# Gate softmax: eight of 32 row tiles of one half of the columns summed with the columns on partitions

## The reference

```
layer 0: x += codebook[argmin distance(gn(x), 1024 codes)]
layer 1: f, g, h = gn(x) @ Wf, Wg, Wh;  x += sigmoid(f g^T per image row) h
layer 2: x0, x1, x2 = gn(x) @ w1, w2, w3                     # one number per pixel each
         sim[n, m] = x0[n] * x1[m];  sm = softmax over n
         feats[m] = sum over n of x2[n] * sm[n, m]
         x += sigmoid(feats) * gn(x)
layer 3: q, k, v = gn(x) @ Wqkv; q softmax over 32, k softmax over 4096 pixels
         out = (k^T v) applied to q, @ w_out + b_out, layer norm;  x += out
```

## Time and profile before

| what | us |
|---|---|
| median of three runs | 5602.64 |
| span of the profiled execution | 5601.4 |
| TensorE busy | 5252.2 |
| VectorE busy | 4106.3 |
| ScalarE busy | 3978.2 |
| GpSimd busy | 1936.0 |

### The profile page before, as it was taken

The page is one execution under the profiler, slowest core; times in us unless marked ns, Lnnn a source line. Parts: engine busy times, 40 slices in busy tenths (PEclk is TensorE's granted clock), DMA queues, the critical chain, the costliest instruction groups (busy, mean ns, idle before and its releaser), DMA issues.

```text
span 5601.4 us, 113931 instructions
## 1 busy us (share of the span) xinstructions
PE 5252.2 (94%) x44520; PEld 2737.7 (49%) x44520; DVE 4106.3 (73%) x8674; ACT 3978.2 (71%) x6023; POOL 1936.0 (35%) x1594
## 2 busy tenths in 40 slices
PE   7799999999999999999999999999999999999996
PEld 3436445363553645446364453645436454463624
DVE  8467777776777777677777777777677777777726
ACT  1467867677785877868677675877858678686795
POOL 3225243342423424233352423424234242433403
PEclk9799999999999999999999999999999999999997
DMA  2010201102011020201102011020110102011000
GB/s 86 9 37 11 68 25 52 37 6 72 20 61 31 13 67 15 64 28 35 48 11 70 23 57 33 15 64 17 61 31 20 61 13 67 26 47 40 7 31 31
DMA packets 163253, 211.22 MB, mean 38 GB/s; under 512 B 13217, under 2 KB 146081, under 8 KB 162721
## 3 DMA queue, kind: packets, MB, share of 16 engines
q1 hardware_dynamic: 138144, 136.79, 7.6%
q0 software_dynamic: 24576, 67.14, 4.1%
HBM read 136.78 MB, written 67.11 MB: 36 GB/s over the span
## 4 chain that ended last, share of the span: by engine, by line
PE 66%; ACT 13%; DVE 11%; issue 6%; POOL 2%; DMA 1%; ACTq 0%; DVEq 0%; SPq 0%; POOLq 0%
PE PS L1195 33%; PE PS L1372 15%; PE PS L1363 6%; ACT n_x L529 3%; DVE stats L849 2%; PE PS L1471 2%; PE PS L1229 2%; PE PS L1253 2%; PE PS L1306 2%; ACT big L601 2%; ACT xin L529 2%; DMA quant_H<-emb_t,idx 1%; ACT work L568 1%; ACT attn L578 1%; ACT soft L601 1%
## 5 line engine op out<-in xcount | busy, mean ns | idle before, releaser
L601 ACT ACTIVATE big<-PS 128x1024 f32<-128x1024 f32 x1376 | 1365.8, 1024 | 460.3 <-PE PS L1363 398.9
L601 ACT ACTIVATE soft<-PS 128x1024 f32<-128x1024 f32 x672 | 676.2, 1024 | 353.9 <-PE PS L1363 346.3
L416 POOL DMA_INDIRECT quant_H<-emb_t,idx x512 | 487.4, 952 | 976.2 <-DVE idx L873 781.2
L1195 PE MATMUL PS<-e_hi,n_hi 128*128 128x512 f16 x2048 | 780.2, 381 | 17.3 <-DVE m L867 9.5
L1195 PE MATMUL PS<-e_hi,n_lo 128*128 128x512 f16 x2048 | 776.7, 379 | 0.0
L1195 PE MATMUL PS<-e_lo,n_hi 128*128 128x512 f16 x2048 | 776.7, 379 | 0.0
L1372 PE MATMUL PS<-big,w 128*4 128x512 f32 x5504 | 756.5, 638 | 0.0
L849 DVE BATCH_NORM_STATS2 stats<-XT 128x6 f32<-128x512 f32 x1024 | 651.7, 683 | 14.5 <-POOL XT L432 4.6
L873 DVE FIND_INDEX8 idx<-m,work 128x8 uint32<-128x1024 f32 x512 | 622.1, 1219 | 0.0
L1363 PE MATMUL PS<-rhs,lhs 12*128 12x512 bf16 x4096 | 557.6, 395 | 61.7 <-ACT big L601 38.8
L867 DVE CUSTOM_DVE_ANT_0 work<-PS,e_bias,m 128x512 f32<-128x512 f32 x512 | 384.0, 750 | 213.2 <-PE PS L1195 189.5
(11 more groups left out here) (208 smaller groups left out, 10799.7 us busy)
## 6 DMA issues: line engine op xcount, KB each, us to landing
xin<-x SPq DMA_DIRECT2D x128, 512.0 KB, 3.9
out<-yout SPq DMA_DIRECT2D x128, 512.0 KB, 2.9
quant_H<-emb_t,idx POOLq DMA_INDIRECT x512
XT<-emb SPq DMA_DIRECT2D x1, 1024.0 KB, 6.2
XT<-wh SPq DMA_DIRECT2D x1, 256.0 KB, 5.8
XT<-wqv SPq DMA_DIRECT2D x1, 256.0 KB, 5.8
XT<-wk SPq DMA_DIRECT2D x1, 128.0 KB, 5.8
w_sb<-w SPq DMA_DIRECT2D x1, 128.0 KB, 5.3
```

The lines of the kernel that those rows point to most:

```text
L416: nc.gpsimd.indirect_dma_start(quant[:, g % 2, u, :], None, emb_t, bass.IndirectOffsetOnAxis(ap=idx[:, t % (2 * GT), 0:1], axis=0),).then_ ...
L601: nc.scalar.activation(E[h % 3][:, z * 1024:(z + 1) * 1024], bank(2 * z, 2), ACT.Exp).then_inc(exped.sem, 1)
L1195: ins = mm(dst, a, b, start=first and j == 0, stop=last and j == 2)
```

## The change

For row tiles 24 to 31 and the second half of the columns (16 column tiles of 128), the products are computed the other way round. The columns m lie on the partitions and 1024 rows n along the free dimension.

- `HALVES` is 56 instead of 64: halves 56 to 63 (two fills, two exponentials, one group of sums each) fall away.
- `rows_out` (SyncE) writes the x0 and x2 values of the last 1024 rows from `rows3` to a DRAM buffer, in two DMAs. `rows_back` reads each back as a row spread over 128 partitions, into `x0_row` and `x2_row` (512 KB each).
- `bexp(im, i)`, 16 per image, on ScalarE: the exponential of `x0_row` with the column's x1 as scale and the negative maximum as bias, both pointers, into `EB`; the denominator comes from the accumulator.
- `bsum(im, i)`, 16 per image, on VectorE: `EB * x2_row`, and its sum is the numerator. All share the one buffer `EB`.
- `extremes` makes `negm`; `gate_chain` adds the 16 sums to those of the matmuls.
- `EB` is `o_x0` and the rows lie over `o_hi` and `o_lo`, the buffers of layer 3; the squares go to a small bf16 buffer; `pk` and `r3` lie over `yout`. `gated(0)` waits for the last `bsum`. `final_z` waits for `l3_qlo` of its own group in the last two groups.
- The lists of the loop on all engines are laid out anew. In the loop six `bexp` stand ahead of the next image's first `l0_norm` and ten behind it; ten `bsum` stand after the first `best`. In the search VectorE takes the next tile's first maximum ahead of the index of the tile before, and `stat1` of groups 5 and 6 and `add0(13)` come after the last index. In the last image `gated(0)` moves behind `gate_chain(0)`.

The diff, without most of the lists:

```diff
-HALVES = 2 * NT
+ROWS = 8
+SIDE = NT // 2
+HALVES = 2 * NT - ROWS
...
+    rows_d = nc.dram_tensor("rows_d", (B, 2, ROWS * P), F32)
...
-        o_hi = sb("o_hi", [P, 2, KC, GW], F16)
-        o_lo = sb("o_lo", [P, 2, KC, GW], F16)
+        o_both = sb("o_both", [P, 2 * GW * KC])
+        o_hi, o_lo = (o_both[:, i * KC * GW:(i + 1) * KC * GW].bitcast(F16).rearrange("p (s k n) -> p s k n", s=2, k=KC)
+                      for i in range(2))
+        x0_row, x2_row = o_both[:, 0:ROWS * P], o_both[:, ROWS * P:2 * ROWS * P]
+        EB = o_x0[:, :, :].rearrange("p k n -> p (k n)")
+        negm = sb("negm", [P, NT])
+        bden = sb("bden", [P, SIDE])
+        bnum = sb("bnum", [P, SIDE])
...
+            def rows_out(im):
+                sp.wait_ge(*rows_kept.after(im, 1))
+                for i in range(2):
+                    sp.dma_start(rows_d[im, i, :].rearrange("(q n) -> q n", q=2),
+                                 rows3[2 * i + 64:P:32, 1, :]).then_inc(rows_sent, 16)
+
+            def rows_back(im):
+                sp.wait_ge(rows_sent, 32 * (im + 1))
+                if im > 0:
+                    sp.wait_ge(*l3_qved.after(im - 1, NG - 1))
+                    sp.wait_ge(*l3_ked.after(im - 1, NG - 1))
+                for i, row in enumerate((x0_row, x2_row)):
+                    sp.dma_start(row, rows_d[im, i, :].partition_broadcast(P)).then_inc(rows_in, 16)
...
+            def bexp(im, i):
+                t = SIDE + i
+                if i == 0:
+                    act.wait_ge(rows_in, 32 * (im + 1))
+                    act.wait_ge(*extremes_done.after(im))
+                    if im > 0:
+                        act.wait_ge(*l3_lo.after(im - 1, NG - 1))
+                act.wait_ge(*b_summed.room(im, i, 1))
+                nc.scalar.activation(EB, x0_row, ACT.Exp, scale=s3[:, 1, t:t + 1], bias=negm[:, t:t + 1],
+                                     accum_out=bden[:, i:i + 1]).then_inc(b_exped.sem, 1)
...
             def gated(im, g):
+                if g == 0:
+                    act.wait_ge(*b_summed.after(im, SIDE - 1))
...
-                v.tensor_tensor(s3[:, 2, :], ma[:, 0, :], ma[:, 1, :], ALU.max).then_inc(extremes_done.sem, 1)
+                link(v.tensor_tensor(s3[:, 2, :], ma[:, 0, :], ma[:, 1, :], ALU.max))
+                v.tensor_scalar(negm[:, :], s3[:, 2, :], -1.0, None, ALU.mult).then_inc(extremes_done.sem, 1)
...
+                v.tensor_copy(nums[:, 0, :, :], turned[:, :, :, 1])
+                link(v.tensor_tensor(nums[:, 1, :, :], turned[:, :, :, 3], side(bden), ALU.add))
+                v.tensor_tensor(gview[:, 1, 1, :, :], turned[:, :, :, 2], side(bnum), ALU.add)
                 link(v.reciprocal(nums[:, :, :, :], nums[:, :, :, :]))
...
+            def bsum(im, i):
+                dve.wait_ge(*b_exped.after(im, i))
+                v.tensor_tensor_reduce(EB, EB, x2_row, 1.0, 0.0, ALU.mult, ALU.add,
+                                       bnum[:, i:i + 1]).then_inc(b_summed.sem, 1)
...
-                if im == B - 1 and c == 2 * NG - 2:
-                    pe.wait_ge(*l3_qlo.after(im, NG - 1))
+                if c >= 2 * NG - 4 and c % 2 == 0:
+                    pe.wait_ge(*l3_qlo.after(im, g))
```

## The result

The changed kernel takes **5513.95 us** (median of 4 runs, 5509.96 to 5522.42) against 5603.25 us before: ratio 0.9847, 95% interval 0.9833 to 0.9861 (the ratio leaves the profiled execution out, so it is not the quotient of the medians, 0.9841). That is 89 us less, where 40 were forecast (5563 us). The direction was right and the time lies in the range, but the gain is more than twice the forecast.

A forecast was written before the change was run, and what follows sets the result against it. ScalarE was taken to bound stage A and the tail, TensorE the search. Fourteen periods x (4.3 - 7.2) = -40.6, image 0 -2.9, tail +3.5: -40.0 us, 5602.6 to 5563 us; range 5490 to 5655.

The forecast's parts named there:

- Removed on TensorE: Stage B: 8 halves an image at 1.25 us, 10.0 us; seven in the search, 8.7; the eighth, filler, worth nothing.
- The search at 115.5 us: First maximum to last index: VectorE's 114.6 us against TensorE's 114.0, the larger counting, plus 0.9 for the shared path.
- the shared path: VectorE and GpSimd block each other: 1.3 of ten `bsum` meet `n_lo` in the search, 0.9 us (bounds 0 and 21).
- Stage B: Halves 32 to 63 beside the codebook search, 140.2 us: forecast -7.2 us (bounds -10.0, TensorE alone, and -1).
- Stage A, +4.3 us: Halves 0 to 31, 82.3 us, bound by ScalarE: six added `bexp` cost +4.3 us (bounds +0.3 and +7.9).
- Stage C, 0: Layers 1 and 3, 115.4 us: orders new, work the same, 0 (bounds -1 and +1 a period).
- The tail, +3.5: Last image's softmax, no search beside it, 144.7 us: ScalarE +4.5 us, 1 us into idle time, so +3.5.
- Rival 1: New orders close ScalarE's idle time, TensorE keeps its whole gain: stage A +1.5, stage B -9.0; 5492 us; chance 0.20.
- Rival 2: One buffer between `bexp` and `bsum` ties ScalarE to VectorE: net +3.1 fifteen times, +50 us, 5653; chance 0.18.
- Rival 3: Each of ten `bsum` in the search meets GpSimd on the shared path at 0.50 us: +35, 5638; chance 0.05.
- Rival 4: Nothing moves: TensorE's saving is exchanged for ScalarE's six `bexp`, stage B -4.6, stage A +4.6: 5603; chance 0.13.
- DMAs: `rows_out` and `rows_back` in SyncE's queue: a 512 KB load lands in 3.9 us, nothing (bounds 0 and one landing a period).

The follow-up runs named there:

- the kernel with four fewer at the end: Changed kernel with four more halves left out, behind the search (52 instead of 56): 5527.13 us (0.9863).
- experiment 4: Changed kernel with the last image in 64 halves, without `bexp` and `bsum`: 5506.05 us, again 5507.26; changed kernel with the last image's fills issued twice: 5541.38 us.
- The kernel with 64 halves: Changed kernel, but the last image's softmax in all 64 halves without `bexp` and `bsum`, in before's orders up to the gate: 5506.05 us, again 5507.26.
- the small `bsum`: Changed kernel with `bsum` working on 8 of its 1024 columns: 5511.45 us (0.9834).

## Why the prediction came out as it did

- **Removed on TensorE, 1.25 us a half: right as a price, too low as a count.** 94 instructions for 10.6 us are 1.35 us for each 12 of them; of the 94, by the records of the search, 60 are sums (7.3 us), 30 fills (2.5) and 4 a turn of gathered rows (0.8). The sums and fills alone are 1.3 us a half. I took seven halves out of the search, 8.7 us; the new orders took out 7.5 and moved a turn behind it, 10.6 us. My count of the sums there, 23 groups to 16, was misread: the records are 200 and 140, 25 groups and 17.5. That the eighth is filler was right in kind, as the kernel with four fewer at the end shows.
- **The search at 115.5 us: this is the term that failed.** I took VectorE as the larger of two equal engines: 101.2 + 12.5 - 3.3 = 110.4 us of work, plus 4.2 us of waits from image 0's search, plus 0.9 for the shared path. Measured: 107.06 us of work and a stretch of 112.1 us that doesn't move when VectorE has 96.9. Ten `bsum` take 11.4 us (1.14 from start to start, 1.22 long, as the read of the sum lies beside the next instruction), and the 64 maxima overlap their neighbours by 2.3 us more than before. The 4.2 us of image 0's search are waits for scores, and I added them as if they were work; that VectorE can do with less is shown only narrowly, by the 3.8 us that it is idle in the 110.54 us of the kernel with four halves struck in the search. TensorE alone was the answer, and at 112.1 us, not my 114.0. So of the 3.4 us that the search was put too long, 1.5 are the wrong engine and 1.9 the count of the line above. Stage B fell by 11.6 us on average, beyond even the bound of -10.0 that I gave for TensorE alone.
- **What that was worth.** Over the fourteen periods the search fell by 10.2 us on average instead of 7.2: 43 us, most of the 53 missed between the profiled executions. What is left of a period, forecast at +4.3, is +3.9 (-6.3 in all, less the search's -10.2), but of other parts than I had it made of. Image 0 brought -10.6 instead of -2.9: its stage A is 1.1 us shorter, not 4.3 longer.
- **Stage A, +4.3 us: +4.5 measured, by another cause; that the number fits is luck.** I had ScalarE's load pay for it. `bexp` does cost 1.22 us from start to start and ScalarE's idle time fell to 3.1 us, near the 4 that I had said. But without the load the stage is as long. The 3.0 us between images 9 and 5 come with the new order, although the clock was at its lower level for 7.3 us of the stage before and for 3.6 after. A line through the fourteen stages A of each kernel, time against time at the lower level, puts them 3.8 us apart at the 9.0 us that before has on average; the other 0.7 us go with 2.5 us more of it. In before's order the load costs 6.3 us: there my mechanism holds, and my price was too low.
- **Stage C, 0: +0.7 us a period** (bound +1), with more of it at the lower clock.
- **TensorE's clock was not in the sum.** The time at the lower of its two levels (1.2 instead of 2.4 GHz) went from 15.8 to 21.2 us a period on average. Within the changed kernel the fourteen periods range from 329.9 us with 13.7 us of it to 338.7 us with 30.7; a straight line through all fourteen has a slope of 0.40 us per microsecond (0.37 in the second profiled execution). By that line, an estimate that takes the clock as the cause, 5.4 us more cost 2.2 us a period, 30 us in all. Set at 13.7 us both, a period goes from 338.4 to 329.7, -8.7 us. With +2.2 that is -6.5; -6.3 was measured.
- **The tail, +3.5: +14.0, in a second profiled execution +9.6**, offset by -6.2 and -6.8 behind it, where I had forecast nothing. My term was ScalarE's 4.5 us of extra work; experiment 4 shows that work to be little of the price, and leaves the order and the clock open. The kernel with 64 halves has the same gain behind its tail (126.1 us against 133.3 before), so it belongs to the new lists or buffers behind the gate; which of them was not tested.
- **Rival 1** (5492 us: A +1.5, B -9.0) was nearest in mechanism and, at 22 us, in time: it had TensorE keep its gain, only with less than there was in B (-11.6 measured) and with A 3 us too cheap. Its objection, two engines near 99% in the search, wasn't needed: VectorE runs at 95%. **Rival 2**, the single buffer: the waits exist (39.0 us in all, 2.4 an image) and cost nothing that can be told, since the small `bsum` gains nothing clear of the noise (ratio 0.9834 against 0.9847, with intervals that overlap). In before's orders the time is ten times that rival's +50 (6104 us), but not by its mechanism: there `bexp` waits for `bsum` 0.4 us in all, and `bsum` for `bexp` 279.5 us, so it is not the wait for the one buffer that costs. **Rival 3**: below. **Rival 4** fell with the time.
- **DMAs**: the rows land in 7.0 us, not 3.9, and nobody waits for them (all 16 waits of `bexp` end with a `bsum`).

## What to carry to other kernels

In a pipeline of in-order queues, ask of each removed instruction whether it stands in the stretch that sets the end: here it was worth its full time inside the search and nothing behind it, and only with orders laid out around its absence. A step added to two queues costs by where it makes them meet as well as by its length (in before's orders 222 us for nearly empty steps, 298 us for their work; in the new ones their work costs next to nothing), so a change that lays its orders anew can't be priced as old time plus new work; measure the new steps emptied before calling an engine the bound. Waits seen on an engine in another stretch are not to be added to its work as a floor.

## What the runs showed of the hardware

**GpSimd is held up by VectorE's product, in this order more often than the other way.** A gather that begins within a `bsum` takes up to 1.85 us instead of 0.95. One such meeting, and the only one of the 256 `bsum` with an `n_lo`, in the timeline of the changed kernel:

```profile
2064.10 1.22 DVE L1007 CUSTOM_DVE_ANT_0 o_x<-o_x,o_both 128x1024 f32<-128x1024 f32 x1
2064.30 1.84 POOL L443 DMA_INDIRECT quant_H<-emb_t,idx  x1 [1.51 <-DVE idx L916]
...
4384.77 2.15 POOL L436 TENSOR_TENSOR n_lo<-n_x,n_hi 128x1024 f16<-128x1024 f32 x1
4385.63 2.38 DVE L1007 CUSTOM_DVE_ANT_0 o_x<-o_x,o_both 128x1024 f32<-128x1024 f32 x1
4387.08 1.78 POOL L443 DMA_INDIRECT quant_H<-emb_t,idx  x1 [0.16 <-PE PS L1314]
```

136 of the 512 gathers overlap a `bsum` and last 1.20 us on average, the other 376 last 0.95; with the small `bsum` all do. In the second case `bsum` starts 0.86 us into the subtraction and stands for its last 1.29 us. So the forecast's "one or two of ten" was one of 256: the new orders keep them apart. In before's orders 60 of 256 overlap an `n_lo`, 44 of them last over 1.3 us, up to 2.9, and `bsum` averages 1384 ns instead of 1222: there the third rival's meetings happen. The Trainium skill, page "SBUF — State Buffer", section "SBUF: two separate sides", tells of an exclusive lock of a shared port pair between the two engines. The trace agrees with that in both directions, at 0.9 us for a gather and 1.16 us for the one `bsum`.

**The lower clock takes a different part of equal periods, and follows no busy share that I could name.** The changed kernel's periods hold between 13.7 and 30.7 us of it, with the same instructions. It begins mostly where a stage starts: in the windows above, 0.90 in one stage A and 0.98 in the next. In the 4 us before the fall of the former TensorE was busy 64%, at the end of layer 3, but the latter comes after the same end, also at 64%, and has no fall there. Where TensorE waits much there is more of it (before's orders with the change: 47.8 us a period), yet more work in the tail brought more too. What sets it stays open, and with it most likely some 20 us of this kernel from one execution to the next: nine of them range from 5501.4 us at a mean granted clock of 0.960 to 5523.3 at 0.954.
